# Products over the states summed in pairs on GpSimd, four product buffers and the product by C in halves, in a Mamba block between two mixtures of experts

## The reference, cut to what matters

```python
def step(h, inp):
    dt_t, B_t, C_t, u_t = inp
    dA = jnp.exp(dt_t[..., None] * A)
    h = h * dA + (dt_t * u_t)[..., None] * B_t[:, None, :]
    y = jnp.einsum('bes,bs->be', h, C_t)
    return (h, y)
...
y = tm(ys) + x_conv * D
y = y * silu(z)
```

## Time and profile before

| | us |
|---|---|
| median of 3 runs | 2282.28 (2280.38 to 2287.38) |
| profiled execution, its own time | 2289.82 |
| its span | 2288.0 |
| TensorE busy | 1871.9 (82%) |
| VectorE busy | 1743.2 (76%) |
| GpSimd busy | 1238.5 (54%) |
| ScalarE busy | 961.1 (42%) |

### The profile page before, as it was taken

How to read it: one execution, slowest core, us unless ns; L and a number is a source line. 1 busy time by engine, 2 the same in 40 slices (tenths; PEclk the granted TensorE clock), 3 DMA queues, 4 the chain that set the end, 5 groups by cost and what they waited for, 6 DMA issues and landing times. The chain is left out here.

```text
span 2288.0 us, 31797 instructions
## 1 busy us (share of the span) xinstructions
PE 1871.9 (82%) x9382; PEld 1309.2 (57%) x9385; DVE 1743.2 (76%) x2734; ACT 961.1 (42%) x1474; POOL 1238.5 (54%) x751
## 2 busy tenths in 40 slices
PE   6289999993696988889888898888675649999996
PEld 6189999991242434334343343434233639999996
DVE  4857666774398989899898898989992577777665
ACT  2323333331545565555655556555441143333331
POOL 1256464564366656566565666656741046555555
PEclk9589999996898999999999999999897559999998
DMA  6244343434243333333333333333320524344332
GB/s 204 81 112 93 70 93 69 84 56 133 81 135 122 120 121 120 120 121 121 120 119 120 121 119 121 122 121 126 125 92 16 169 83 82 81 82 92 82 75 29
DMA packets 160981, 237.44 MB, mean 104 GB/s; under 512 B 29370, under 2 KB 85296, under 8 KB 160304
## 3 DMA queue, kind: packets, MB, share of 16 engines
q1 hardware_dynamic: 130096, 198.84, 27.3%
q0 software_dynamic: 30720, 36.53, 9.6%
HBM read 202.57 MB, written 38.34 MB: 105 GB/s over the span
## 5 line engine op out<-in xcount | busy, mean ns | idle before, releaser
L1192 POOL TENSOR_TENSOR m_dB<-m_DTU,m_BC 128x1024 f32<-128x1024 f32 x256 | 603.1, 2358 | 388.7 <-DVE PS L1293 388.2
L1293 DVE TENSOR_TENSOR_SCAN PS<-PS,m_ST,m_dB 128x512 f32<-128x512 f32 x512 | 631.1, 1278 | 107.2 <-POOL m_dB L1192 44.8
L1017 PE MATMUL PS<-m_G,keep_ident 128*128 128x512 f32 x1024 | 516.8, 630 | 145.8 <-DVE m_G L1303 145.3
L1025 ACT ACTIVATE PS<-m_DT,m_A 128x512 f32<-128x512 f32 x512 | 347.2, 689 | 316.0 <-DVE PS L1293 311.6
L1017 PEld LDWEIGHTS PS<-m_G,keep_ident 128*128 128x128 f32 x1024 | 190.3, 197 | 422.9 <-DVE m_G L1303 247.5
L1303 DVE TENSOR_TENSOR m_G<-PS,m_BC 128x1024 f32<-128x1024 f32 x256 | 313.2, 1223 | 23.9 <-issue 2.7
L603 PE MATMUL PS<-e_xh,e_wh 128*128 128x256 f32 x1008 | 294.5, 292 | 0.5 <-DVEq L491 0.3
L603 PE MATMUL PS<-e_xl,e_wh 128*128 128x256 f32 x1008 | 288.7, 286 | 0.0
L603 PE MATMUL PS<-e_xh,e_wl 128*128 128x256 f32 x1008 | 288.2, 286 | 0.0
L621 PE MATMUL PS<-e_wh,e_hh 128*128 128x256 f32 x1008 | 281.2, 279 | 0.0
L621 PE MATMUL PS<-e_wl,e_hh 128*128 128x256 f32 x1008 | 280.6, 278 | 0.0
(11 more groups left out here) (194 smaller groups left out, 2801.4 us busy)
## 6 DMA issues: line engine op xcount, KB each, us to landing
m_BC<-bc_rows SPq DMA_DIRECT2D x512, 256.0 KB, 3.3
layer_raw<-w SPq DMA_DIRECT2D x64, 512.0 KB
xrows<-r_xn SPq DMA_DIRECT2D x16, 512.0 KB, 4.4
keep_X<-x SPq DMA_DIRECT2D x4, 1024.0 KB, 9.3
sums<-keep_X SPq DMA_DIRECT2D x4, 1024.0 KB, 11.1
out<-keep_X SPq DMA_DIRECT2D x4, 1024.0 KB, 11.0
keep_X<-sums SPq DMA_DIRECT2D x3, 1024.0 KB, 13.3
e_xin<-xrows,e_gix POOLq DMA_INDIRECT x160
```

The costliest lines, as they stand in the source:

```text
L1017: last = M(PS[:, B_Y + j, :], C["ident"][:, :], G[:, s % 2, j, :], start=False, stop=(s == DS - 1))
L1025: return nc.scalar.activation(out, in_, func, **kw)
L1192: G_.tensor_tensor(dB[:, s % 2, :, :], DTU[:, es, :], BC[:, s % NBC, 0:1, :].to_broadcast([P, 2, CT]), ALU.mult).then_inc(dB_ok, 1)
L1293: V.tensor_tensor_scan(PS[:, B_H + j, :], PS[:, B_DA + j, :], dB[:, s % 2, j, :], ST[:, s, e:e + 1], ALU.mult, ALU.add).then_inc(scanned, 1)
```

## The change

G has four buffers. Of each four steps n % 4 = 0 and 1 are read by TensorE as before. For steps 2 and 3 GpSimd adds the product of step 3 to that of step 2 in place (`add_up`), and TensorE, at step 3, reads the sum: six products of 512 columns where eight were. GpSimd's addition for a four stands in its queue two steps later, behind the dB product of step n % 4 = 1; the last one of a turn stands at step 1 of the next.

VectorE's product by C is two operations of 512, the first ahead of the state copy and the second behind it. A scan waits for the product of its own half of the step before. The gating product moves from step 0 (16) to step 1 (17), and the back items out, squares, v, hr, T and xa move later by one or two steps (from `(1,_,2,_)` to `(2,_,4,_)` for the first).

```diff
-        G = sb("G", [P, 2, 2, CT])
+        NG = 4
+        G = sb("G", [P, NG, 2, CT])
...
+        READS = 3 * (STEPS // NG)
+
+        def reads(n):
+            return 3 * (n // NG) + (1, 2, 2, 3)[n % NG]
+
+        def pairs(n):
+            return n // NG + 1
...
-            ("out", 0): (1, _, 2, _), ("out", 1): (3, _, 4, _), ("sq", 0): (_, 5, _, _), ("v", 0): (_, _, 6, 8),
-            ("hr", 0): (_, 9, _, _), ("T", 0): (10, 10, _, _), ("T", 1): (12, 12, _, _), ("xa", 0): (_, _, _, 11), ("xa", 1): (_, _, _, 13),
+            ("out", 0): (2, _, 4, _), ("out", 1): (4, _, 6, _), ("sq", 0): (_, 7, _, _), ("v", 0): (_, _, 8, 10),
+            ("hr", 0): (_, 11, _, _), ("T", 0): (12, 12, _, _), ("T", 1): (14, 14, _, _), ("xa", 0): (_, _, _, 13), ("xa", 1): (_, _, _, 15),
...
-                        pe.wait_ge(g_ok, k * STEPS + (n + 1))
-                        for j in range(2):
-                            last = M(PS[:, B_Y + j, :], C["ident"][:, :], G[:, s % 2, j, :], start=False, stop=(s == DS - 1))
-                        last.then_inc(g_read, 1)
+                        if n % NG < 2:
+                            for j in range(2):
+                                pe.wait_ge(g_ok, k * (2 * STEPS) + (2 * n + j + 1))
+                                last = M(PS[:, B_Y + j, :], C["ident"][:, :], G[:, n % NG, j, :], start=False, stop=False)
+                            last.then_inc(g_read, 1)
+                        elif n % NG == 3:
+                            pe.wait_ge(pair_ok, k * (STEPS // NG) + pairs(n))
+                            for j in range(2):
+                                last = M(PS[:, B_Y + j, :], C["ident"][:, :], G[:, 2, j, :], start=False, stop=(s == DS - 1))
+                            last.then_inc(g_read, 1)
...
+            def add_up(k, n):
+
+                gp.wait_ge(g_ok, k * (2 * STEPS) + 2 * (n + 1))
+                G_.tensor_tensor(G[:, 2, :, :], G[:, 2, :, :], G[:, 3, :, :], ALU.add).then_inc(pair_ok, 1)
...
+                        if n % NG == 1 and n > 1:
+                            add_up(k, n - 2)
+                        elif n == 1 and not is_first(k):
+                            add_up(k - 1, STEPS - 1)
                         items(ON_POOL, n, k, par, has_front, has_back, front, back)
...
-                        if not (is_first(k) and n == 0):
-                            dve.wait_ge(kept, k * STEPS + n)
                         for j in range(2):
                             e = 2 * p + j
+                            if not (is_first(k) and n == 0):
+                                dve.wait_ge(g_ok, k * (2 * STEPS) + (2 * n + j - 1))
+                                dve.wait_ge(kept, k * STEPS + n)
...
-                        if s == 0 and p == 1:
+                        if s == 1 and p == 1:
                             gated(k, 0, par)
-                        elif s == 0 and has_back:
+                        elif s == 1 and has_back:
                             gated(k - 1, 1, 1 - par)
...
+                        def weigh(j):
+                            dve.wait_ge(scanned, k * (2 * STEPS) + (2 * n + j + 1))
+                            V.tensor_tensor(G[:, n % NG, j, :], PS[:, B_H + j, :], BC[:, s % NBC, 1, :], ALU.mult).then_inc(g_ok, 1)
+
                         dve.wait_ge(c_in[s % NBC], k * (16 * STEPS // NBC) + 16 * (n // NBC + 1))
+                        if not (is_first(k) and n < NG):
+                            if n % NG == 3:
+                                dve.wait_ge(pair_ok, k * (STEPS // NG) + pairs(n - NG))
+                            else:
+                                dve.wait_ge(g_read, k * READS + reads(n - NG + (1 if n % NG == 2 else 0)))
+                        weigh(0)
                         dve.wait_ge(scanned, k * (2 * STEPS) + (2 * n + 2))
...
                         V.tensor_tensor(ST[:, s, 2 * p:2 * p + 2].bitcast(U32), PS[:, B_H:B_H + 2, CT - 1].bitcast(U32),
                                         mask[:, bass.ds(k + 1, 1)].to_broadcast([P, 2]), ALU.bitwise_and).then_inc(kept, 1)
+                        weigh(1)
```

More of the change, by code:

```diff
@@ L820, in mamba @@
         dA_ok, dB_ok, scanned, g_ok, g_read, kept = (sem(n) for n in ("dA_ok", "dB_ok", "scanned", "g_ok", "g_read", "kept"))
+        pair_ok = sem("pair_ok")
         yz_ok, xn_ok, sq_ok, v_ok, rs_ok, hr_ok, q_ok, xa_ok = (sem(n) for n in (
@@ L914, in load @@
                 n = p * DS + s
-                for j, landed, used in ((0, b_in, dB_ok), (1, c_in, g_ok)):
+                for j, landed, used, each in ((0, b_in, dB_ok, 1), (1, c_in, g_ok, 2)):
                     if n >= NBC or not is_first(k):
-                        sp.wait_ge(used, k * STEPS + (n - NBC + 1))
+                        sp.wait_ge(used, k * (each * STEPS) + each * (n - NBC + 1))
                     src = bc_dram[bass.ds(k, 1), j, s:s + 1, :].rearrange("o q t -> (o q) t")
@@ L1059, in front @@
                         act.wait_ge(dtu_ok, k * 2 - 2)
-                        act.wait_ge(g_read, k * STEPS - (2 * STEPS - DS - 1))
+                        act.wait_ge(g_read, k * READS - (2 * READS - reads(DS)))
                     F(U[:, par, n, :], f_bank(k, p), ACT.Identity, bias=mc[:, n, C_CB:C_CB + 1]).then_inc(f_r, 1)
@@ L1193, in turn @@
                                          ALU.mult).then_inc(dB_ok, 1)
+                        if n % NG == 1 and n > 1:
+                            add_up(k, n - 2)
+                        elif n == 1 and not is_first(k):
+                            add_up(k - 1, STEPS - 1)
                         items(ON_POOL, n, k, par, has_front, has_back, front, back)
-            run(gp, turn, front, back, lambda: None)
+            run(gp, turn, front, back, lambda: add_up(MCH - 1, STEPS - 1))
         @block.vector
@@ L1258, in gated @@
                 dve.wait_ge(sz_ok, k + 1)
-                dve.wait_ge(g_read, k * STEPS + (p + 1) * DS)
+                dve.wait_ge(g_read, k * READS + reads((p + 1) * DS - 1))
                 if p == 0 and not is_first(k):
```

## The result

The changed kernel takes 2401.0 us (median of 4, 2389.3 to 2405.1) where the kernel before takes 2282.8 (median of 4): a ratio of 1.0507, 95% interval 1.0465 to 1.0549. It is slower by 118 us. I had forecast slower, 2342 us, and a range up to 2382; the direction was right, the size half of what came.

What follows compares the result with a forecast made beforehand. VectorE's own chain (scans, weighing by C, state copy, bubble) was taken as the bound. Six turns at +9.7 us (58), first turn +2, last -2, end +2 gave +60 on 2282.3: 2342 us, range 2258 to 2382.

Steps and rivals of the forecast that it cites:

- VectorE's own saving: VectorE's scan step with C product in halves: 0.41 us a step saved in the loop, 0.26 outside; alone 95 us.
- TensorE's fewer products: TensorE's identity products: 48 a turn for 64, 13.8 us a turn less work, worth nothing by itself.
- SyncE's rows: SyncE's loads of the rows of B and C: they land well before they are wanted, cost nothing.
- The new wait: TensorE's wait for GpSimd's sum: pair there 4.8 us after the step's second scan, where the plain product came at 1.3.
- the gate: Gating product moved to steps 1 and 17, waiting for the last pair: starts at 8.5 us where it was at 4.0.
- The stretches 0 to 3 and 3 to 9: Scan 0 to 3 and scan 3 to 9 of a loop turn: longer by 4.5 and 3.8 us.
- Steps 9 to 20: Scan 9 to scan 20 of a loop turn: 52.8 us for 48.9, +3.9, from c2, z2, z3 and the SiLUs.
- Steps 20 to 32: End of a loop turn: small delays at dt and GpSimd, otherwise the new pace; 47.5 us for 49.7, -2.2.
- Outside the loop: First turn +2 us, last turn -2, end gate +2.
- The half clock: TensorE at half clock after idling: in the carried turn, 3.4 us for the pair ahead of the gate.
- rival C: Half clock behind idle stretches at each of 8 pairs a turn: 9 us a turn on top, 2396 us; chance 0.08.
- Rival A: VectorE's saving comes through as lighter TensorE catches up: -6 us a turn, 2236 us, 2187 without stalls; chance 0.20.

Runs made afterwards that it cites:

- e1: Against the kernel before: only VectorE's product by C in halves, with four product buffers; no GpSimd sum, gate and back items unmoved; 2237.0 us, ratio 0.9763.
- e3: Changed kernel without GpSimd's sum and its wait; TensorE reads three products of four, each third state's product is missing from y; 2310.0 us, ratio 1.0085.
- e2: Changed kernel with TensorE reading all products plainly and no GpSimd sum, gate and back items still moved; 2304.5 us, ratio 1.0056.
- e6: Changed kernel with VectorE's sum of the last output product (pj 1) at step 31 in place of 30; 2375.2 us, ratio 1.0371.
- e5: Changed kernel with four products of a zero matrix ahead of each of TensorE's waits for a pair; 2376.8 us, ratio 1.0381.

## Why the prediction was wrong in size

By its own steps:

**VectorE's own saving: right.** 3.64 us forecast, 3.61 to 3.63 measured, and covered waits cost nothing. But e1 shows that this saving could never reach the chain whole: 4.3 of 14 us a turn did. **TensorE's fewer products worth nothing: right** (e3 against e2). **SyncE's rows: nothing, as said**; the views of waits list none for them.

**The new wait, and the gate: right, and shown.** The pair came at E(n) + 4.8: the scans of step 31 end at 905.13 (902.67 + 2.46, the scan before 906.29 is at 902.67) and the pair starts at 909.97. The same 4.8 holds for the pairs of steps 3 to 23 in that turn. The gate starts 7.5 us after scan 0 for 7.3 by hand, though TensorE had idled for 6.36 us ahead of the pair and not for 9. The stretches 0 to 3 and 3 to 9 were 0.9 and 0.1 us from what I carried, the second by errors that cancel: in the turn shown, scans 6 and 7 (938.80 and 946.31), behind T1 and x0, were late by 1.9 and 3.2 us for 1.1 and 2.4, and the variance (955.31) by 1.7 for about 2.6 that is left for it in the carried value.

**Steps 9 to 20: 2.1 us a turn too low.** I put z2 behind the gate with the skip at full clock, though I had it at a part-slow clock at step 0. The trace has it at 3.78 at step 17 too, and scan 19 waited 4.00 us for a forecast 1.8:

```profile
988.69 2.52 PE L1034 MATMUL PS<-m_G,keep_ident 128*128 128x512 f32 x4 [2.73 <-POOL m_G L1203]
992.63 3.78 PE L1025 MATMUL PS<-m_U,m_skip 128*128 128x512 f32 x4 [1.41 <-DVE m_T L1289]
```

**Steps 20 to 32: "the rest runs at the new pace" is the step that failed.** 52.5 for 47.5, of which the loop's jump, in the measured means alone, is 0.7; 4.3 us a turn, 26 in six. Behind the pair of step 27 stood product 28 and the second output product (pj 1), and VectorE's sum for it kept its step 30, since the change moved the back items up to step 14 and left those from step 20 on. I had priced GpSimd's lateness here only for dB (0.3 and 1.0, which came as 0.3 and 0.9), not for the pair: behind du and dB it came 8.1 us after the scans of step 27 and not 4.8, and then ran at half clock. At the end of the turn before the one shown:

```profile
889.32 2.35 POOL L1203 TENSOR_TENSOR m_G<-m_G 128x1024 f32<-128x1024 f32 x1
```

```profile
891.72 3.78 PE L1034 MATMUL PS<-m_G,keep_ident 128*128 128x512 f32 x4 [3.54 <-POOL m_G L1203]
895.29 3.15 PE L1029 MATMUL PS<-m_G,keep_ident 128*128 128x512 f32 x4
898.28 3.62 PE L1003 MATMUL PS<-m_MW,m_HID 128*128 128x256 f32 x16
```

VectorE wanted it at 897.7 and began at 902.06, 4.35 us late; over the six turns this wait is 21.9 us. e6, which moves VectorE's sum by one step, gets 31 us back, 23 of them in the six turns.

**Outside the loop: +21 for +2.** Six turns give 6 x 15.7 = 94 us of the 115 by which the span grew. The first turn took 140.5 for 132.6 (+8, forecast +2), the last 133.1 for 128.9 to its scan 31 (+4, forecast -2), the end gate came 4.1 us later after it (forecast 2). Behind the gate the output product ran at half clock, 5.66 us for 3.69 (2 us), and 3 us lie ahead of scan 0, where nothing was changed. I had costed the outer turns from three items. In the first turn scans waited 2.62 us (at 636.25) and 3.50 us (at 726.72) for ScalarE at places where I had counted nothing.

**The half clock was priced once, and as a rival after that.** I gave rival C 9 us a turn on top and a chance of 0.08. The waits of 3.54, 4.17, 5.23 and 6.36 us in the rows above are each followed by records at half clock. The Trainium skill, "TensorE: Matmul & The Clock Gate", section "Why this matters for your kernels", has that idle gaps between bursts lose the fast clock; these rows agree. Filling at the pairs gives 29 us back alone, but only 7 on top of e6, where it also costs delays of its own. So the slow clock belonged into the times of step 17 and of pj, as a term and not as a rival; whether it costs through ScalarE the 54 us of rival C stays open, since the filling gives and takes there. The share of the clock at the gate isn't in these numbers (VectorE reads the bank of y there, so filling wasn't tried).

In the profiled executions the span grew by 115 us for a forecast of 60. Of the 55 between, 36 lie in the six turns (5.0 us a turn in the last stretch, 2.1 from 9 to 20, less 1.0 in the first two) and 19 outside. The cause of the largest part, pj behind the late and slow pair of step 27, is shown by e6 and e5. The 2.1 at step 17 and the outer turns are read from the traces; no run separates those. Rival A, that a lighter TensorE would let the chain catch up, fell: e3 is no faster than e2.

## What to carry to other kernels

When work moves from one in-order engine to another, price the wait that it adds by everything queued behind it: here 1.72 us less on TensorE per four steps bought a wait of 3.5 us (169.1 us at the 48 pairs of six turns), and behind it stood what ScalarE and then VectorE needed next. Carry the queue through the whole period, the quiet end too, and where items stand behind a long wait of TensorE, take their times at the slow clock. When an engine gets faster, first ask how much room the engine that feeds it has left: here, in e1, about half of the saving turned into waits for it. Test the parts of a bundle alone: the halves were worth 54 us, and the sum and its moved gate threw 170 away.

## What the runs showed of the hardware that was not expected

TensorE went to half clock after an idle stretch of 2.43 us, but ran at full clock after 2.17 us (e1's skip) and after 2.92 us before a pair of the changed kernel. So the length of the stretch alone doesn't decide:

```profile
1029.43 1.98 PE L1034 MATMUL PS<-m_G,keep_ident 128*128 128x512 f32 x4 [2.92 <-POOL m_G L1203]
```

Products of a zero matrix in the idle stretches raised the granted clock from 0.88 to 0.96 (e5), so work without content held it up too. And GpSimd's sum of 1024 columns took 2348 ns, as long as its product of the same shape (2354). VectorE's operations showed no slowing by it: a scan took 1277 ns on average, 1278 before, and the two scans at 906.29, with the sum at 907.58 beside them, their usual 2.46 us.
